# Windowed attention in a transformer kernel: the mask moved from a TensorE matmul to a VectorE addition, the maximum's subtraction to GpSimd, with new orders of work on four engines

## The chip, the cores and the metric

The kernel runs on one core of a Trainium2 chip. The metric is the device time of one execution in microseconds (us). A core has a matrix engine (TensorE; PE in the rows, PEld for its weight loads), VectorE (DVE), ScalarE (ACT), GpSimd (POOL) and SyncE (SP), which here issues the transfers. Each engine works through its own list of instructions in order; between engines only semaphores set an order.

## The reference

The input is 16 sequences of 256 tokens with 128 features. A layer norm is followed by two branches whose results are added to the input: a delta-rule mixer (untouched by the change) and a transformer of six layers, which takes most of the time. Its attention, cut to what matters (16 heads of 64, windows of 32 queries that see their own and the window before):

```python
sim = einsum('bhwie,bhwje->bhwij', bq, bk2) * QK_SCALE      # 32 queries x 64 keys a window
sim = where(mask, -finfo.max, sim)                          # mask: causal, at most 32 back, none before token 0
attn = softmax(sim, -1)
out = einsum('bhwij,bhwje->bhwie', attn, bv2)
x = attn_layer(shift_tokens(x), ...) + x
x = ffn_layer(shift_tokens(x), ...) + x
```

Queries and keys are normalised to length 1 a head and rotated before the scores are formed.

## The kernel before

`local_transformer` runs six layers over 16 sequences as one software pipeline. Each sequence of a layer is an item, and one body of the pipeline handles five items in different stages, the newest first: `new`, `turn`, `att`, `out`, `ffn`. `pipeline` calls the engine's `body` 16 times a layer and four times at the end. What each engine does in a body, and in which order, is a list written out by hand in that engine's `body` function; a step that waits holds everything behind it in the list.

The steps, by stage:

- Projection: `query_key` multiplies the item by a 512-wide piece of the weights, chunks 0 to 7, each as three matmuls into the one bank `ps_proj` (L1402). VectorE rotates it with two multiplications (`rotate` part 0 and 1, L1228 and L1235), ScalarE squares it (`square`, L1066), and only then may TensorE write chunk c + 1. VectorE sums the squares (`sum_squares`, L1243), GpSimd adds the two halves of the rotation (`add`, L987).
- Norms: when all eight chunks are summed, `inverse_roots` makes the inverse square roots on VectorE for the queries and keys of one item and for the layer norm of another at once: two preparing operations (L1292, L1295) and eleven Newton steps, one waiting for the other (`newton_step`, L61 to L69). GpSimd multiplies by them (`scale`, L997), TensorE turns the result (`turn_qk`, L1437), ScalarE copies it out (`turned_out`, L1077). `spread` on TensorE (L1527) hands the layer norm's roots out over the partitions, and `deviate`, `affine` and `ffn_in` follow it.
- Values: `value` makes four projections (pieces n = 0 to 3) into the bank `ps_p`, `value_out` copies each to the buffer `v` (L1088). After the fourth, SyncE issues 16 transfers that spread `v` over windows into `vw` (`window`, L935). There is one `v`: `value_out(x, before, 0)` of the next item waits until all 16 transfers of the item before have landed (semaphore `vw_in`).
- Attention: an item has four units. `score` writes a unit's scores into one of two banks: first a matmul of the identity by the mask (L1448), which writes the mask into the bank, then 32 small products accumulated onto it (L1454, 64 instructions in the trace). VectorE takes the negated maximum from the bank (`top`, L1251) and adds it while it copies the scores to the SBUF buffer `pr` (`shift`, L1260). ScalarE takes the exponential (`exp`, L1097), VectorE the sum and its reciprocal (`total`, L1269 and L1272), GpSimd normalises (`norm`, L1006), TensorE turns the probabilities (`turn_probs`, L1469, bank `ps_p`), ScalarE copies them (`probs_out`, L1106), TensorE multiplies by the values (`weigh`, L1487), ScalarE copies that out (`heads_out`, L1115).
- Rest of the layer: `join_heads` (L1502), `attended` (L1279), `shift_state` (L1124), `mean` (L1510), `centre` (L1286), `square_centred` (L1132), `variance` (L1518), then `spread`, `deviate`, `affine`, `ffn_in` (L1541), `gelu` (L1148), `hidden` (L1317), `ffn_out` (L1550), `layer_out` (L1325).

ScalarE's `gelu` and the first `exp` behind it each load their function table (ACT_TABLE_LOAD). Three bodies a layer also convert weights (`b.switch` of -2, -1 and 1).

## Time and profile before

| | us |
|---|---|
| median of 3 runs | 4424.85 (4423.68 to 4428.69) |
| profiled execution | 4430.44 |
| its span, first to last instruction | 4428.3 |

| engine | busy us | share of the span |
|---|---|---|
| PE | 4003.8 | 90% |
| PEld | 3348.1 | 76% |
| DVE | 3420.2 | 77% |
| ACT | 2492.3 | 56% |
| POOL | 2303.8 | 52% |

The share of busy time is an average over the span. The first projection of the transformer starts 729.1 us after the span's start and the last at 4338.6 us, so about 3,600 us belong to the pipeline described above and the first 700 us to the mixer.

### The profile page before, as it was taken

Reading aid. Unit: us, or ns where it says so; the run is one execution under the profiler, and the core shown is the slowest. Engines: PE = TensorE matmul, PEld = TensorE weight load, DVE = VectorE, ACT = ScalarE, POOL = GpSimd, SP = SyncE. Lnnn points to the kernel's source line nnn. Section 1 sums busy time; section 2 is a strip of 40 time slices with the busy share of each in tenths; the row PEclk is TensorE's granted clock in tenths of the full one; section 3 lists DMA queues with packets and bytes.
Section 4 is the critical chain, followed back from the end, with each engine's and each line's share of the span. In section 5 each row is a group of like instructions: output and inputs, shape, how many; then the busy total and the mean of one; then the engine's idle time right before and its main releaser. Section 6 shows DMA issues by size and latency. Waiting matters only on the chain. (4 is left out here: it accounts for less than half of the span.)

```text
span 4428.3 us, 165233 instructions
## 1 busy us (share of the span) xinstructions
PE 4003.8 (90%) x71312; PEld 3348.1 (76%) x71312; DVE 3420.2 (77%) x6567; ACT 2492.3 (56%) x4423; POOL 2303.8 (52%) x2141
## 2 busy tenths in 40 slices
PE   4746743899999999999999999999999999999997
PEld 4635531688888888878888888888788888888885
DVE  4376565788888888888888888888888888888883
ACT  2322211466666666666666666666666666666663
POOL 1000002566656666666666666666666665666661
PEclk9766655899999999999999999999999999999998
DMA  1000000222222222222222222222222222222222
GB/s 57 22 12 12 2 12 34 71 56 56 56 56 57 71 56 57 56 57 71 56 56 56 56 66 71 56 56 56 66 71 56 56 56 53 64 55 57 53 57 64
DMA packets 133868, 232.99 MB, mean 53 GB/s; under 512 B 26640, under 2 KB 36624, under 8 KB 131472
## 3 DMA queue, kind: packets, MB, share of 16 engines
q1 hardware_dynamic: 133136, 222.32, 20.6%
q8 instruction: 571, 9.36, 1.0%
q14 instruction: 161, 1.32, 0.1%
HBM read 29.28 MB, written 4.19 MB: 8 GB/s over the span
## 5 line engine op out<-in xcount | busy, mean ns | idle before, releaser
L987 POOL TENSOR_TENSOR qk<-rot_a,rot_b 128x512 f32<-128x512 f32 x768 | 983.5, 1285 | 418.7 <-PE bank L1437 378.2
L997 POOL TENSOR_TENSOR qk<-qk,rn 128x512 f32<-128x512 f32 x768 | 801.5, 1049 | 216.0 <-DVE rn L69 206.1
L1487 PEld LDWEIGHTS bank<-pT,vw 64*64 64x64 f32 x24576 | 752.3, 136 | 100.5 <-issue 99.5
L1487 PE MATMUL bank<-pT,vw 64*64 64x32 f32 x24576 | 794.9, 220 | 0.7 <-ACT pT L1106 0.7
L1006 POOL TENSOR_TENSOR pr<-pr,prec 128x512 f32<-128x512 f32 x384 | 400.2, 1042 | 706.1 <-DVE prec L1272 705.9
L1228 DVE TENSOR_TENSOR rot_a<-bank,rot 128x512 f32<-128x512 f32 x768 | 529.4, 689 | 297.6 <-PE bank L1402 296.4
L1066 ACT ACTIVATE sq<-bank 128x512 f32<-128x512 f32 x768 | 457.5, 596 | 470.4 <-DVE rot_b L1235 465.0
L1402 PE MATMUL bank<-w_hi,xs_hi 128*128 128x512 f32 x1152 | 555.3, 482 | 77.7 <-ACT sq L1066 28.2
L1243 DVE TENSOR_REDUCE ss<-sq 128x8 f32<-128x512 f32 x768 | 509.6, 664 | 139.0 <-ACT sq L1066 139.0
L1235 DVE TENSOR_TENSOR rot_b<-bank,rot 128x512 f32<-128x512 f32 x768 | 522.9, 681 | 0.0
L1437 PE MATMUL bank<-ident,qk 128*128 128x128 f32 x3072 | 472.6, 277 | 4.9 <-POOL qk L997 4.7
L1402 PE MATMUL bank<-w_hi,xs_lo 128*128 128x512 f32 x1152 | 461.8, 401 | 0.0
L1402 PE MATMUL bank<-w_lo,xs_hi 128*128 128x512 f32 x1152 | 460.5, 400 | 0.0
L1454 PEld LDWEIGHTS bank<-kT,qT 64*32 64x32 f32 x24576 | 363.5, 107 | 116.8 <-issue 116.7
L1437 PEld LDWEIGHTS bank<-ident,qk 128*128 128x128 f32 x3072 | 386.1, 145 | 81.5 <-POOL qk L997 9.3
L1454 PE MATMUL bank<-kT,qT 64*32 64x64 f32 x24576 | 426.9, 219 | 1.2 <-issue 0.9
L1088 ACT ACTIVATE v<-bank 128x512 f32<-128x512 f32 x384 | 229.1, 597 | 278.3 <-PE bank L1402 274.2
L1502 PE MATMUL bank<-oT,wo 128*128 128x256 f32 x1536 | 347.2, 379 | 0.7 <-ACT oT L1115 0.7
L1106 ACT ACTIVATE pT<-bank 128x512 f32<-128x512 f32 x384 | 229.2, 597 | 192.2 <-PE bank L1469 192.2
L1077 ACT ACTIVATE kT<-bank 128x512 f32<-128x512 f32 x384 | 228.1, 594 | 191.9 <-PE bank L1437 191.2
L1402 PEld LDWEIGHTS bank<-w_hi,xs_hi 128*128 128x128 f32 x1152 | 221.2, 192 | 137.0 <-issue 52.1
L1502 PEld LDWEIGHTS bank<-oT,wo 128*128 128x128 f32 x1536 | 291.5, 190 | 43.3 <-ACT oT L1115 0.8
(238 smaller groups left out, 6724.6 us busy)
## 6 DMA issues: line engine op xcount, KB each, us to landing
vw<-v SPq DMA_DIRECT2D x1344, 128.0 KB
vw<-v SPq DMA_DIRECT2D x192, 64.0 KB
stage<-in_wqkv SPq DMA_DIRECT2D x6, 1536.0 KB, 6.1
stage<-in_wb_all SPq DMA_DIRECT2D x6, 1088.0 KB, 5.3
d_band<-in_band SPq DMA_DIRECT2D x8, 512.0 KB, 5.3
d_xt<-in_x SPq DMA_DIRECT2D x4, 512.0 KB, 4.1
base_scratch<-d_res SPq DMA_DIRECT2D x4, 512.0 KB, 3.0
o_base<-base_scratch SPq DMA_DIRECT2D x1, 2048.0 KB, 8.4
```

Of the source, the lines that this page charges most:

```text
L987: nc.gpsimd.tensor_tensor(qk[:, c, :], rot_a[:, c % 2, :], rot_b[:, c % 2, :], ALU.add)\
L997: nc.gpsimd.tensor_tensor(y, y, rn[:, x.q, 8 * c:8 * c + 8].unsqueeze(2).to_broadcast([P, 8, DH]), ALU.mult).then_inc(S["scaled"], 1)
L1006: nc.gpsimd.tensor_tensor(y, y, prec[:, k % 2, :].unsqueeze(2).to_broadcast([P, NPAIR, KEYS]), ALU.mult).then_inc(S["normed"], 1)
L1066: nc.scalar.activation(sq[:, :], ps_proj[:, :], ACT.Square).then_inc(S["squared"], 1)
L1228: nc.vector.tensor_tensor(rot_a[:, c % 2, :].rearrange("p (h d) -> p h d", h=8), ps_proj[:, :].rearrange("p (h d) -> p h d", h=8), cos, AL ...
L1235: nc.vector.tensor_tensor(rot_b[:, c % 2, :].rearrange("p (h a d) -> p h a d", h=8, a=2), y[:, :, ::-1, :], sin, ALU.mult).then_inc(S["rot ...
L1243: nc.vector.tensor_reduce(ss[:, 8 * c:8 * c + 8], sq[:, :].rearrange("p (h d) -> p h d", h=8), AX.X, ALU.add).then_inc(S["summed"], 1)
L1402: mm = nc.tensor.matmul(out[:, :], x[:, q, half * P:(half + 1) * P], w[:, cols:cols + CK], start=n == 0, stop=n == 2)
L1437: mm = nc.tensor.transpose(ps_turn[:, i * P:(i + 1) * P], qk[:, c, i * P:(i + 1) * P], ident[:, :])
L1454: mm = nc.tensor.matmul(bank[w * WIN:(w + 1) * WIN, h * KEYS:(h + 1) * KEYS], qT[rows, x.q, h, q0:q0 + WIN], kT[rows, x.q, h, q0:q0 + KEYS ...
L1487: mm = nc.tensor.matmul(ps_o[rows, c * P + w * WIN:c * P + (w + 1) * WIN], vw[rows, x.q, 4 * half + w, first:first + DH], pT[rows, k % 2, ...
L1502: mm = nc.tensor.matmul(ps_c[:, 0:L], wo[:, c, :], oT[:, x.q, c, :], start=c == 0, stop=c == NPAIR - 1)
```

## The change

The mask is no longer written by a matmul. The first small product of `score` overwrites the bank. A new VectorE step `masked` adds the mask (now in SBUF, 128 x 64, repeated for eight heads) to the scores while copying them to `pr`; `top` takes the negated maximum from `pr`; `shift` moves to GpSimd, where it adds the negated maximum to `pr` in place. `score` waits for `masked` of the unit that had the bank before, where it waited for `shift`.

Beside that the lists of all four compute engines are in a new order, and the ends of the bodies lie elsewhere: the last chunk's rotation, `centre` and `inverse_roots`, which opened VectorE's body, now close the body before; ScalarE's `shift_state`, `square(7)`, `square_centred` and the fourth `value_out` do likewise, and TensorE scores unit 0 of `turn` at the end of a body in place of unit 0 of `att` at its start. The identity in bfloat16 is dropped with its preparation. The diff, cut to its core:

```diff
@@ -997,6 +995,15 @@
                 nc.gpsimd.tensor_tensor(y, y, rn[:, x.q, 8 * c:8 * c + 8].unsqueeze(2).to_broadcast([P, 8, DH]),
                                         ALU.mult).then_inc(S["scaled"], 1)
 
+            def shift(x, k):
+
+                if not x.there:
+                    return
+                need(pool, S["maxed"], x.u * 4 + (k + 1))
+                y = pr[:, k % 2, :, :]
+                nc.gpsimd.tensor_tensor(y, y, negmax[:, k % 2, :].unsqueeze(2).to_broadcast([P, NPAIR, KEYS]),
+                                        ALU.add).then_inc(S["shifted"], 1)
+
             def norm(x, k):
 
...
@@ -1012,25 +1019,29 @@
                     low_half(new, "added", turn.u * 8 + 7)
                 else:
                     low_half(new, "prepared", NPREP)
-                scale(att, 7)
+                shift(out, 3)
                 scale(turn, 0)
-                scale(turn, 1)
                 add(turn, 7)
                 add(new, 0)
+                scale(turn, 1)
                 scale(turn, 2)
+                shift(att, 0)
+                norm(out, 3)
                 add(new, 1)
+                norm(att, 0)
                 scale(turn, 3)
-                norm(out, 3)
+                add(new, 2)
+                shift(att, 1)
+                add(new, 3)
                 scale(turn, 4)
-                add(new, 2)
-                norm(att, 0)
-                add(new, 3)
                 norm(att, 1)
                 scale(turn, 5)
                 add(new, 4)
+                shift(att, 2)
+                scale(turn, 6)
                 add(new, 5)
                 norm(att, 2)
-                scale(turn, 6)
+                scale(turn, 7)
                 add(new, 6)
 
...
@@ -1150,16 +1161,6 @@
 
             def body(b):
                 new, turn, att, out, ffn = b.items
-                shift_state(ffn)
-                square(turn, 6)
-                heads_out(out, 0)
-                probs_out(out, 1)
-                turned_out(att, 5)
-                square_centred(ffn)
-                value_out(att, out, 3)
-                if b.switch == -1:
-                    convert(b, (4, 5), (S["v_projected"], turn.u * 4))
-                square(turn, 7)
                 if b.switch == -2:
                     convert(b, (0, 2, 1, 3), (S["projected"], new.u * 8))
                 high_half(b, new)
@@ -1168,38 +1169,48 @@
                     need(act, S["wo_done"], out.u)
                     nc.scalar.activation(wo[:, :, :].rearrange("p c n -> p (c n)"), stage_wo, ACT.Copy)\
                         .then_inc(S["conv_act"], 1)
-                turned_out(att, 6)
+                if b.switch == -1:
+                    convert(b, (4, 5), (S["v_projected"], turn.u * 4))
+                probs_out(out, 2)
                 heads_out(out, 1)
-                probs_out(out, 2)
                 turned_out(att, 7)
+                affine(ffn)
                 square(new, 0)
                 turned_out(turn, 0)
+                exp(out, 3)
+                gelu(ffn)
+                square(new, 1)
+                value_out(turn, att, 0)
+                exp(att, 0)
+                turned_out(turn, 1)
+                square(new, 2)
+                probs_out(out, 3)
                 heads_out(out, 2)
-                affine(ffn)
-                exp(out, 3)
-                turned_out(turn, 1)
-                square(new, 1)
-                gelu(ffn)
                 turned_out(turn, 2)
-                square(new, 2)
-                value_out(turn, att, 0)
-                probs_out(out, 3)
-                exp(att, 0)
+                value_out(turn, att, 1)
                 square(new, 3)
+                probs_out(att, 0)
+                exp(att, 1)
                 turned_out(turn, 3)
-                exp(att, 1)
-                heads_out(out, 3)
-                value_out(turn, att, 1)
-                turned_out(turn, 4)
                 square(new, 4)
-                probs_out(att, 0)
-                square(new, 5)
-                exp(att, 2)
                 value_out(turn, att, 2)
                 if b.switch == 1:
                     need(act, S["y_done"], ffn.u + 1)
                     nc.scalar.activation(w1[:, :, :, :].rearrange("p a c n -> p (a c n)"), stage_w1, ACT.Copy)\
                         .then_inc(S["conv_act"], 1)
+                heads_out(out, 3)
+                turned_out(turn, 4)
+                square(new, 5)
+                exp(att, 2)
+                heads_out(att, 0)
+                square(new, 6)
+                probs_out(att, 1)
+                turned_out(turn, 5)
+                shift_state(out)
+                value_out(turn, att, 3)
+                square(new, 7)
+                square_centred(out)
+                turned_out(turn, 6)
 
             pipeline(body)
...
@@ -1243,23 +1254,24 @@
                 nc.vector.tensor_reduce(ss[:, 8 * c:8 * c + 8], sq[:, :].rearrange("p (h d) -> p h d", h=8),
                                         AX.X, ALU.add).then_inc(S["summed"], 1)
 
-            def top(x, k):
-
-                if not x.there:
-                    return
+            def masked(x, k):
+
+                if not x.there:
+                    return
+                half, e = unit(k)
                 need(dve, S["scored"], x.u * 4 + (k + 1))
-                nc.vector.tensor_reduce(negmax[:, k % 2, :], ps_s[k % 2][:, :].rearrange("p (h n) -> p h n", h=NPAIR),
-                                        AX.X, ALU.max, negate=True).then_inc(S["maxed"], 1)
-
-            def shift(x, k):
-
-                if not x.there:
-                    return
-                need(dve, S["maxed"], x.u * 4 + (k + 1))
                 need(dve, S["p_turned"], x.u * 4 + (k - 1))
                 nc.vector.tensor_tensor(pr[:, k % 2, :, :], ps_s[k % 2][:, :].rearrange("p (h n) -> p h n", h=NPAIR),
-                                        negmax[:, k % 2, :].unsqueeze(2).to_broadcast([P, NPAIR, KEYS]), ALU.add)\
-                    .then_inc(S["shifted"], 1)
+                                        mask[:, half, :].unsqueeze(1).to_broadcast([P, NPAIR, KEYS]), ALU.add)\
+                    .then_inc(S["masked"], 1)
+
+            def top(x, k):
+
+                if not x.there:
+                    return
+                need(dve, S["masked"], x.u * 4 + (k + 1))
+                nc.vector.tensor_reduce(negmax[:, k % 2, :], pr[:, k % 2, :, :], AX.X, ALU.max, negate=True)\
...
@@ -1327,11 +1339,6 @@
 
             def body(b):
                 new, turn, att, out, ffn = b.items
-                centre(ffn)
-                rotate(turn, 7, 0)
-                rotate(turn, 7, 1)
-                sum_squares(turn, 7)
-                inverse_roots(turn, ffn)
                 if b.switch == -2:
                     need(dve, S["loaded_a"], b.layer * 32 + 32)
                     need(dve, S["rotated"], new.u * 16)
...
-                rotate(new, 0, 0)
-                top(out, 3)
-                rotate(new, 0, 1)
                 if b.switch == -1:
                     convert(b, (4, 5), 4)
+                rotate(new, 0, 0)
                 deviate(ffn)
-                shift(out, 3)
+                rotate(new, 0, 1)
+                masked(att, 0)
+                top(att, 0)
                 sum_squares(new, 0)
                 rotate(new, 1, 0)
                 rotate(new, 1, 1)
                 total(out, 3)
                 sum_squares(new, 1)
-                top(att, 0)
+                hidden(ffn)
                 rotate(new, 2, 0)
-                shift(att, 0)
                 rotate(new, 2, 1)
+                total(att, 0)
+                sum_squares(new, 2)
+                rotate(new, 3, 0)
+                rotate(new, 3, 1)
+                masked(att, 1)
                 top(att, 1)
-                hidden(ffn)
-                rotate(new, 3, 0)
-                sum_squares(new, 2)
-                rotate(new, 3, 1)
-                shift(att, 1)
-                total(att, 0)
                 sum_squares(new, 3)
                 rotate(new, 4, 0)
+                masked(att, 2)
                 rotate(new, 4, 1)
...
-                total(att, 1)
                 sum_squares(new, 4)
                 rotate(new, 5, 0)
                 rotate(new, 5, 1)
                 top(att, 2)
-                shift(att, 2)
                 sum_squares(new, 5)
-                if b.switch == 1:
-                    need(dve, S["conv_dve"], b.layer * 2 + 2)
-                attended(out)
+                masked(att, 3)
                 rotate(new, 6, 0)
                 rotate(new, 6, 1)
                 total(att, 2)
                 sum_squares(new, 6)
+                if b.switch == 1:
+                    need(dve, S["conv_dve"], b.layer * 2 + 2)
+                attended(out)
+                rotate(new, 7, 0)
+                rotate(new, 7, 1)
+                centre(out)
+                top(att, 3)
+                sum_squares(new, 7)
+                inverse_roots(new, out)
 
             pipeline(body)
...
@@ -1443,17 +1455,15 @@
                     return
                 half, e = unit(k)
                 need(pe, S["turned_out"], x.u * 8 + (4 * half + 4))
-                need(pe, S["shifted"], x.u * 4 + (k - 1))
+                need(pe, S["masked"], x.u * 4 + (k - 1))
                 bank = ps_s[k % 2]
-                nc.tensor.matmul(bank[:, :].rearrange("p (h n) -> p h n", h=NPAIR), ident_b[:, :],
-                                 mask[:, half, :].unsqueeze(1).to_broadcast([P, NPAIR, KEYS]), start=True, stop=True)
                 rows = slice(e * DH, (e + 1) * DH)
                 for h in range(NPAIR):
                     for w in range(4):
                         q0 = half * P + w * WIN
                         mm = nc.tensor.matmul(bank[w * WIN:(w + 1) * WIN, h * KEYS:(h + 1) * KEYS],
                                               qT[rows, x.q, h, q0:q0 + WIN], kT[rows, x.q, h, q0:q0 + KEYS],
-                                              start=False, stop=True, skip_group_check=True)
+                                              start=True, stop=True, skip_group_check=True)
                 mm.then_inc(S["scored"], 1)
...
@@ -1553,48 +1563,48 @@
             def body(b):
                 new, turn, att, out, ffn = b.items
                 query_key(b, new, 0)
-                turn_qk(att, 7)
+                value(b, turn, 0)
+                spread(ffn)
+                score(att, 1)
+                turn_qk(turn, 0)
+                ffn_in(ffn, 1)
+                ffn_in(ffn, 0)
+                query_key(b, new, 1)
                 weigh(out, 2)
-                spread(ffn)
-                turn_qk(turn, 0)
-                score(att, 0)
-                query_key(b, new, 1)
+                ffn_in(ffn, 2)
                 turn_qk(turn, 1)
-                ffn_in(ffn, 0)
-                ffn_in(ffn, 1)
-                value(b, turn, 0)
                 query_key(b, new, 2)
+                score(att, 2)
                 turn_qk(turn, 2)
-                score(att, 1)
-                ffn_in(ffn, 2)
+                turn_probs(out, 3, turn, 0)
+                query_key(b, new, 3)
+                value(b, turn, 1)
+                ffn_out(ffn)
+                turn_probs(att, 0, turn, 1)
+                query_key(b, new, 4)
                 turn_qk(turn, 3)
-                query_key(b, new, 3)
-                turn_probs(out, 3, turn, 0)
-                ffn_out(ffn)
                 weigh(out, 3)
-                query_key(b, new, 4)
-                value(b, turn, 1)
+                value(b, turn, 2)
+                score(att, 3)
+                query_key(b, new, 5)
                 turn_qk(turn, 4)
-                score(att, 2)
-                turn_probs(att, 0, turn, 1)
-                query_key(b, new, 5)
+                weigh(att, 0)
+                turn_qk(turn, 5)
+                turn_probs(att, 1, turn, 2)
+                query_key(b, new, 6)
                 join_heads(b, out)
-                turn_qk(turn, 5)
-                query_key(b, new, 6)
-                value(b, turn, 2)
-                weigh(att, 0)
-                turn_probs(att, 1, turn, 2)
+                query_key(b, new, 7)
+                value(b, turn, 3)
                 if b.switch == 1:
                     need(pe, S["conv_act"], b.layer * 2 + 2)
                     need(pe, S["conv_dve"], b.layer * 2 + 2)
                 mean(out)
-                query_key(b, new, 7)
-                value(b, turn, 3)
+                score(turn, 0)
+                turn_qk(turn, 6)
                 variance(out)
-                turn_qk(turn, 6)
                 turn_probs(att, 2, turn, 3)
+                turn_qk(turn, 7)
                 weigh(att, 1)
-                score(att, 3)
 
             pipeline(body)
```

## Rows read from the trace of the kernel before

**Rows 1.** Busy time in a stretch: us, then busy us and count by engine, PEclk.

```profile
1660.00:2220.00 560.00, 553.99 (x9570) 466.06 (x9566) 463.92 (x902) 362.55 (x650) 354.01 (x329) 0.99 0.25 59
```

**Rows 2.** Timeline of TensorE: start us, duration us, line, operation; `spread` of two consecutive bodies.

```profile
2151.08 0.71 PE L1527 MATMUL bank<-ident,rn 128*128 128x128 f32 x4
...
2187.88 0.71 PE L1527 MATMUL bank<-ident,rn 128*128 128x128 f32 x4
```

**Rows 3.** Line L1169 (once a layer): shortest/median/longest ns, first and last start.

```profile
L1169 ACT ACTIVATE wo<-stage x5: 1057/1057/1057, 1433.3 to 3829.6; 128x1024 f32<-128x1024 f32 x5
```

**Rows 4.** Timeline of TensorE in one body, each block from its start to the next.

```profile
2162.11 1.56 PE L1550 MATMUL bank<-hid,w 128*128 128x256 f32 x6
2163.60 2.06 PE L1487 MATMUL bank<-pT,vw 64*64 64x32 f32 x64
2165.59 0.50 PE L1402 MATMUL bank<-w_hi,xs_hi 128*128 128x512 f32 x1
...
2167.09 0.60 PE L1437 MATMUL bank<-ident,qk 128*128 128x128 f32 x4
2167.52 0.38 PE L1448 MATMUL bank<-mask,ident_b 128*128 128x512 bf16 x1
2167.83 1.10 PE L1454 MATMUL bank<-kT,qT 64*32 64x64 f32 x64
2168.86 0.66 PE L1469 MATMUL bank<-ident,pr 128*128 128x128 f32 x4
...
2170.05 3.62 PE L1502 MATMUL bank<-oT,wo 128*128 128x256 f32 x16
2173.50 0.60 PE L1437 MATMUL bank<-ident,qk 128*128 128x128 f32 x4
```

**Rows 5.** Timeline of VectorE: the `shift` of one unit.

```profile
2152.34 0.68 DVE L1260 TENSOR_TENSOR pr<-bank,negmax 128x512 f32<-128x512 f32 x1
```

**Rows 6.** Costliest groups on the page: busy us, mean ns of one | idle before.

```profile
L1006 POOL TENSOR_TENSOR pr<-pr,prec 128x512 f32<-128x512 f32 x384 | 400.2, 1042 | 706.1 <-DVE prec L1272 705.9
```

**Rows 7.** Timeline of TensorE and VectorE: projection of chunk 7, last Newton step.

```profile
2178.15 0.58 PE L1402 MATMUL bank<-w_hi,xs_hi 128*128 128x512 f32 x1
...
2186.86 0.23 DVE L69 SCALAR_TENSOR_TENSOR rn<-rn_t,rn 128x66 f32<-128x66 f32 x1
```

**Rows 8.** Timeline of GpSimd and VectorE: Newton steps beside GpSimd's work and without.

```profile
2182.35 0.72 POOL L975 TENSOR_TENSOR xs_lo<-stateT,xs_hi 64x256 fp32r<-64x256 f32 x1
...
2182.43 0.69 DVE L61 TENSOR_SCALAR rn_t<-ss 128x66 int32<-128x66 int32 x1
...
1913.96 0.20 DVE L61 TENSOR_SCALAR rn_t<-ss 128x66 int32<-128x66 int32 x1
...
1915.74 0.65 DVE L69 SCALAR_TENSOR_TENSOR rn<-rn_t,rn 128x66 f32<-128x66 f32 x1
```

**Rows 9.** Timeline of SyncE: the 16 transfers of `window`, in two bodies.

```profile
2143.76 14.10 SPq L935 DMA_DIRECT2D vw<-v  x16
...
2217.34 11.85 SPq L935 DMA_DIRECT2D vw<-v  x16
```

**Rows 10.** Short stretches behind them, columns as Rows 1, then DMA share and GB/s.

```profile
2159.00:2159.40 0.40, 0.40 (x44) 0.40 (x32) 0.40 (x2) 0.33 (x1) 0.40 (x2) 1.00 0.31 72
2159.40:2160.38 0.98, 0.98 (x20) 0.81 (x9) 0.98 (x2) 0.50 (x2) 0.98 (x2) 1.00 0.00 0
...
2230.75:2235.00 4.25, 4.25 (x84) 3.43 (x83) 3.62 (x7) 3.24 (x7) 4.24 (x4) 1.00 0.00 0
```

**Rows 11.** Timeline of ScalarE: `value_out` of piece 0, a table load, the next-but-one operation.

```profile
2160.38 0.59 ACT L1088 ACTIVATE v<-bank 128x512 f32<-128x512 f32 x1
...
2162.89 1.28 ACT L1097 ACT_TABLE_LOAD   x1
...
2164.72 0.58 ACT L1066 ACTIVATE sq<-bank 128x512 f32<-128x512 f32 x1
```

**Rows 12.** A stretch at a change of layer, columns as Rows 10.

```profile
1920.00:1921.00 1.00, 0.38 (x1) 0.41 (x2) 1.00 (x2) 0.00 (x0) 1.00 (x1) 0.50 0.86 201
```

14 lines of the change are left out of this document (7 added, 7 removed).

## The prediction

> **What bounds the kernel now.** I read the busy time of a long stretch first. In 560 us of the pipeline TensorE is busy for 554 us at a granted clock of 0.99, VectorE for 464, ScalarE for 363, GpSimd for 354 [rows 1]. So TensorE sets the time, and what counts is how long one body keeps it. Next, two consecutive starts of `spread`: they lie 36.80 us apart [rows 2], and ordinary bodies repeat that number. A layer takes (3829.6 - 1433.3) / 4 = 599.1 us [rows 3], which is 16 x 36.80 = 588.8 us and 10.3 us for the change of weights. Then the timeline of one body block by block [rows 4]: each block of TensorE begins where the last one lets it, with no wait between them. The present order is thus limited by TensorE's work alone, and every other wait in the profile is cover. The question is whether this stays so.
>
> **What the change removes.** In front of each of the 4 units of a body the mask matmul goes. From its start to the start of the scores behind it are 0.31 us [rows 4]. Not all of that is its own. The six 512-wide matmuls of two projections start 1.50 / 6 = 0.25 us apart, and that includes what the first one waits [rows 4]; the mask is as wide. Some 0.21 us are the matmul, and 0.10 us the passage from full tiles to the narrow tiles of the scores, which the kernel still makes. So 4 x 0.21 = 0.85 us leave a body, and TensorE's own work falls to 35.95 us; the other end is 4 x 0.31 = 1.24 us, 35.6 us. My sum of the new list by the blocks of [rows 4] gives 36.1 us. I use 36.0.
>
> **What it adds and moves.** VectorE: `masked` reads a bank and one SBUF operand and writes 128 x 512, as `shift` did at 0.68 us [rows 5], so it costs the same; `top` reads SBUF in place of a bank, also some 0.68 us. Where the two stand side by side the second waits for the first, 0.1 us each, twice a body in place of once. GpSimd gains 4 subtractions of one operand by a broadcast one, the form of `norm` at 1.04 us [rows 6]: 4.2 us a body, on an engine that is busy for 354 / 560 x 36.80 = 23.3 us. It ends at 27.4 of 36, so it is no bound; `exp` gets its scores about a microsecond later, and I find no matmul waiting for that. All of this is cover and costs nothing on the path. The dropped identity saves one copy in the preparation, under 1 us.
>
> The price lies in the new lists. I walk the new body with t = 0 at the start of the projection of chunk 7 on TensorE.
>
> First, **the Newton steps.** `spread` waits for `inverse_roots`. Before, from the projection of chunk 7 (2178.15) to the end of the last Newton step (2186.86 + 0.23) are 8.94 us, and `spread` starts at 2187.88 [rows 2, 7], 0.79 us later: free. In the new order VectorE has the same rotations, `centre` behind them and one reduction more (`top(att, 3)`), partly in the wait for the square; I get 9.05 us. TensorE meanwhile gets to `spread` earlier: chunk 7 0.89, value 0.70, mean 0.53, score 1.03, turn 0.43, variance 0.43, turned probabilities 0.41, turn 0.53, weigh 1.99, chunk 0 0.80, value 0.70, together 8.4 us ([rows 4], with 0.10 for each passage to narrow tiles; 0.89 and 0.53 are my estimates for a projection and a mean beside full 4-byte matmuls). It waits 0.6 us a body. What stretches the Newton steps is GpSimd: L61 takes 0.69 us beside GpSimd's operation that starts 0.08 us before it, 0.20 us with GpSimd idle, and L69, elsewhere 0.23 us, takes 0.65 us beside GpSimd [rows 7, 8]. In the new list the same three GpSimd operations (two halves of `low_half`, then `shift(out, 3)` for `scale(att, 7)`) fall on the Newton steps, so their delay of some 1.8 us stays. If it did not, 9.05 would be 7.2 and the wait would vanish; if it grew by one operation, the wait would be 1.6 us. The Trainium skill (SBUF — State Buffer, Who interferes with whom) says that GpSimd shares a port pair with VectorE, that a VectorE instruction with two SBUF inputs or in a two-port mode is locked out for the whole of a GpSimd instruction, and that one with at most one SBUF input is not. By that rule, the trace agrees (0.20 against 0.69 us), `masked` and `top` take no harm from the four new GpSimd operations.
>
> Second, **the transfers of the values.** `value_out` of the fourth piece ends and SyncE starts 2143.76 - (2178.15 - 36.80) = 2.4 us after chunk 7 [rows 2, 7, 9]; in the new list this step has the same neighbours, so again at 2.4. The 16 transfers need until 2159.40 in one body (15.6 us after the start: DMA share 0.31 before, 0.00 behind) and until 2230.75 at the latest in another (13.4 us) [rows 9, 10]. Seven successive bodies that I read this way lie between 13.0 and 15.6 us, these two near the ends; the middle is 14.1. `value_out` of the next item's first piece overwrites `v` and waits for them. Before, it starts at 2160.38 [rows 11], 16.6 us after SyncE's start: just covered. In the new list it stands two places further ahead, behind `square(new, 1)`; the walk brings ScalarE there at t = 15.6 (`spread` 9.1, `deviate` and `affine` to 10.9, `gelu` with its load to 15.1, `square` to 15.7). The transfers land at t = 2.4 + 14.1 + 0.1 = 16.6. [...]
>
> Behind the waiting `value_out` on ScalarE stand the table load for `exp`, `exp(att, 0)`, `turned_out(turn, 1)` and `square(new, 2)`. From the start of `value_out`: 0.6, then from the load to the operation behind `exp` 1.83 us (2162.89 to 2164.72) [rows 11], then 0.6 for `turned_out`, 3.1 us with the hand-over. TensorE needs it for `turn_qk(turn, 2)`, which so starts at t = 16.6 + 3.1 = 19.7. From there TensorE's list runs through to the next chunk 7: turn 0.43, turned probabilities 0.41, chunk 3 and value 1.50, `ffn_out` 1.49, turned probabilities and chunk 4 1.19, turn 0.53, weigh 1.99, value 0.90, score 1.03, chunk 5 0.80, turn 0.53, weigh 1.99, turn 0.43, turned probabilities and chunk 6 1.19, `join_heads` 3.45, together 17.9 us [rows 4]. The body closes at 19.7 + 17.9 = 37.6 us. That loop passes by the Newton wait, so the two are not added. With transfers of 13.0 us it would be 36.5 (then the next bound holds), with 15.6 us 39.1.
>
> If the transfers were in time, the loop over the Newton steps would hold: 36.0 + 0.6 for `spread`, and a further 0.2 to 0.3 for chunk 3, since its square comes behind exp's table load. That is near 36.9; I write 37.0.
>
> **The sum.** 37.6 - 36.8 = 0.8 us in about 90 ordinary bodies is +72 us. The bodies with a change of weights hide these waits behind their own (TensorE stands before chunk 0 and then runs at half its clock [rows 12]), some 1 us less a layer: -6 us. The filling and draining of the pipeline I take as unchanged. 4430.4 + 66 = 4496 us for the profiled execution. This lies 5.6 us above the median of the runs, so the forecast for the median is 4424.85 + 66 = 4491 us.
>
> **The rivals.**
> (1) Forecast, the transfers of the values are not in time and ScalarE waits: 4491 us, its own range 4450 to 4560 us by the bounds of the transfers. For it: the place moves ahead by 3.4 us where 1.0 to 3.6 us were free. Chance 0.50.
> (2) Not slower: nothing waits, TensorE's work alone counts. This needs the Newton steps at under 8.4 us (GpSimd's three operations beside other work) and transfers of at most 13 us or an earlier start. Then 36.0 to 36.3 us a body, -0.5 to -0.8 us in 96 bodies: 4345 to 4377 us. For it: TensorE runs without a wait now, and the mask's time is truly taken away. Against it: both walks. Chance 0.21.
> (3) Only the Newton wait: 37.0 us a body, +18 - 6 = +12 us, 4437 us, 4415 to 4449. Chance 0.20.
> (4) The clock falls. At a change of layer the granted clock is 0.50, 1.2 of 2.4 GHz, after TensorE stood for 4.5 us [rows 12]; if waits of about a microsecond did that in each body, some 4.5 us more a body would give about 4890 us. Over a long stretch with small gaps it was 0.99 [rows 1]. Chance 0.04.
> (5) The change does not shorten the softmax: exp comes a GpSimd operation later and TensorE waits at the turned probabilities too, 0.3 us more a body, 4520 us. Chance 0.05.
>
> **How the numbers follow.** The likeliest is (1), 4491 us. The range, 4350 to 4550 us, leaves out (4), the end of (1) with transfers of over 15 us in every body, and the fast end of (2), about 0.15 together. A measurement here tells 0.2% (9 us) from no change, so 4416 to 4434 is "same": half of (3), little of the others, 0.12. Faster: (2) and a little of (3), 0.22. Slower: 0.66.
>
> **What the profile of the changed kernel would show.** Starts of `spread` 37.6 us apart (36.0 for (2), 37.0 for (3)). TensorE idle before `turn_qk`, put down to ScalarE's copy, about a microsecond a body, and ScalarE idle before `value_out` of piece 0 with a transfer as releaser; TensorE idle before `spread`, put down to L69's successor, about 0.6 us. No L1448; scores still about 0.1 us behind a full tile. GpSimd's busy time up by 384 x 1.04 = 400 us, VectorE's unchanged within 20 us. Newton steps of up to 1 us in the middle of the chain. The prediction is wrong if the transfers start earlier than 2.4 us after chunk 7 or take less time, if VectorE gets through the Newton steps between GpSimd's operations, or if a block of TensorE costs otherwise in its new neighbourhood.

## The result and the profile after

| | before | after |
|---|---|---|
| median of 4 runs, us | 4426.77 (4423.68 to 4430.06) | 4510.94 (4503.61 to 4517.69) |
| span of the profiled execution, us | 4428.3 | 4512.5 |
| ordinary body, us | 36.80 | 37.55 |
| layer, us | 599.1 | 612.8 |

The kernel is slower: ratio 1.019, 95% interval 1.017 to 1.021. The forecast was 4491 us and 37.6 us a body. Where the body gets its length is another matter, and most of what follows is about that.

Busy time of the stretch of [rows 1], same columns:

```profile
1660.00:2220.00 560.00, 540.82 (x9350) 450.77 (x9351) 460.46 (x888) 361.16 (x637) 404.92 (x378) 0.98 0.25 60
```

TensorE is busy for 13 us less than before, at nearly the same clock (0.98, before 0.99): it waits now. GpSimd has 51 us more in it. The whole span, on the page of after, against VectorE's 3420.2 and GpSimd's 2303.8 us before:

```profile
PE 4001.3 (89%) x70928; PEld 3320.9 (74%) x70928; DVE 3461.4 (77%) x6567; ACT 2527.5 (56%) x4423; POOL 2702.8 (60%) x2524
```

Two starts of `spread` (now L1537), as in [rows 2]; the brackets give the idle time before it and what ended it:

```profile
2169.53 0.71 PE L1537 MATMUL bank<-ident,rn 128*128 128x128 f32 x4 [0.85 <-DVE rn L69]
...
2207.08 0.71 PE L1537 MATMUL bank<-ident,rn 128*128 128x128 f32 x4 [0.85 <-DVE rn L69]
```

They are 37.55 us apart, and in front of each TensorE is idle until the last Newton step. Before, `spread` stood there with no wait. The layer, as in [rows 3]: (3889.2 - 1437.9) / 4 = 612.8 us.

```profile
L1170 ACT ACTIVATE wo<-stage x5: 1057/1057/1057, 1437.9 to 3889.2; 128x1024 f32<-128x1024 f32 x5
```

The waits between 1200 and 4300 us (who waited <- for whom: total us, times, longest us) say which one repeats in each body. PEld and PE are the weight load and the matmul of the same operation, so their two waits are one:

```profile
PEld bank L1537 <- DVE rn L69: 91.8, 71, 1.6
...
PE bank L1537 <- DVE rn L69: 60.9, 71, 1.1
...
PEld bank L1520 <- ACT xf L1136: 33.7, 75, 0.5
...
PEld bank L1414 <- ACT sq L1077: 19.5, 63, 0.7
...
ACT v L1099 <- DMA vw<-v: 8.4, 17, 2.2
```

The Newton steps hold `spread` 71 times. The transfers, on which the forecast stood, hold `value_out` only 17 times, 8.4 us in all.

Now the chain that ends in `spread`, in the body that begins at 2159.63 with the projection of chunk 7 (t = 0). TensorE, GpSimd and VectorE, in order of time within each:

```profile
2159.63 0.58 PE L1414 MATMUL bank<-w_hi,xs_hi 128*128 128x512 f32 x1
...
2163.84 1.27 POOL L985 TENSOR_TENSOR qk<-rot_a,rot_b 128x512 f32<-128x512 f32 x1 [3.04 <-PE bank L1449]
2165.26 0.72 POOL L973 TENSOR_TENSOR xs_lo<-stateT,xs_hi 64x256 fp32r<-64x256 f32 x1
2166.06 0.63 POOL L975 TENSOR_TENSOR xs_lo<-stateT,xs_hi 64x255 fp32r<-64x255 f32 x1
2166.77 1.04 POOL L1004 TENSOR_TENSOR pr<-pr,negmax 128x512 f32<-128x512 f32 x1
...
2164.34 0.83 DVE L61 TENSOR_SCALAR rn_t<-ss 128x66 int32<-128x66 int32 x1
2165.20 0.20 DVE L63 TENSOR_SCALAR rn<-rn_t 128x66 int32<-128x66 int32 x1
2165.43 0.64 DVE L65 TENSOR_TENSOR rn_t<-rn 128x66 f32<-128x66 f32 x1
2166.11 0.67 DVE L67 SCALAR_TENSOR_TENSOR rn_t<-rn_t,ss 128x66 f32<-128x66 f32 x1
2166.81 1.08 DVE L69 SCALAR_TENSOR_TENSOR rn<-rn_t,rn 128x66 f32<-128x66 f32 x1
...
2169.25 0.23 DVE L69 SCALAR_TENSOR_TENSOR rn<-rn_t,rn 128x66 f32<-128x66 f32 x1
```

Four of the first five Newton steps take 0.64 to 1.08 us, where a step that GpSimd doesn't delay takes 0.20 to 0.23. Each long one lies beside one of four GpSimd operations. I had counted three (the two halves of `low_half` and the new subtraction). The fourth is `add(new, 6)`, L985: it overwrites piece 6 of `qk`, so it waits until `turn_qk(turn, 6)` has read the old one, and GpSimd stands idle for 3.04 us until then. It starts at 2163.84, half a microsecond ahead of the first Newton step. The last step ends at t = 9.85.

The transfers of the same body, and `value_out` of the next item's first piece:

```profile
2162.03 11.09 SPq L934 DMA_DIRECT2D vw<-v  x16
...
2176.14 0.59 ACT L1099 ACTIVATE v<-bank 128x512 f32<-128x512 f32 x1
```

SyncE starts at t = 2.40. ScalarE comes to `value_out` at t = 16.51 and waits for nothing. The DMA share is 0.00 from 2175.50 on, so the traffic was over 0.6 us before.

A second difference lies in the bodies with a change of weights. TensorE waited there once a layer, for 4.1 to 4.5 us; now it waits for 3.8 us and, a body later, for another 2.24 us. In each of these waits the granted clock falls to its lower level, 1.2 of 2.4 GHz, and stays there for 4 to 11 us. The second wait, and the stretch behind it (columns as [rows 10]):

```profile
1976.58 0.76 PE L1414 MATMUL bank<-w_hi,xs_hi 128*128 128x512 f32 x1 [2.24 <-DVE w_lo L1227]
...
1975.50:1986.00 10.50, 9.42 (x85) 7.85 (x86) 5.85 (x10) 4.18 (x7) 6.99 (x6) 0.51 0.73 205
```

It is `value` of piece 0, which now stands second in TensorE's body. In such a body it needs weights that VectorE converts (L1227), and VectorE comes to that only behind the Newton steps: with those shortened, as in the first experiment below, the wait falls to 0.5 us.

### The profile page after: what moved, and what is told of

Read it like the earlier page. It is cut to its first block and busy times, and to the rows that moved or that the text cites. A ratio compares the mean times of both kernels' runs of the same rounds, so it can differ in the third digit from the quotient of the medians.

```text
span 4512.5 us, 164941 instructions
## 1 busy us (share of the span) xinstructions
PE 4001.3 (89%) x70928; PEld 3320.9 (74%) x70928; DVE 3461.4 (77%) x6567; ACT 2527.5 (56%) x4423; POOL 2702.8 (60%) x2524
## 5 line engine op out<-in xcount | busy, mean ns | idle before, releaser
L985 POOL TENSOR_TENSOR qk<-rot_a,rot_b 128x512 f32<-128x512 f32 x768 | 985.3, 1283 | 488.2 <-PE bank L1449 465.5
L1414 PE MATMUL bank<-w_hi,xs_hi 128*128 128x512 f32 x1152 | 568.4, 493 | 86.9 <-POOL xs_lo L975 25.3
L1449 PE MATMUL bank<-ident,qk 128*128 128x128 f32 x3072 | 490.7, 283 | 17.5 <-ACT kT L1088 11.7
L1004 POOL TENSOR_TENSOR pr<-pr,negmax 128x512 f32<-128x512 f32 x384 | 402.9, 1049 | 54.8 <-DVE negmax L1273 35.2
L1449 PEld LDWEIGHTS bank<-ident,qk 128*128 128x128 f32 x3072 | 349.2, 142 | 102.4 <-issue 33.9
L1108 ACT ACTIVATE pr<-pr 128x512 f32<-128x512 f32 x384 | 241.9, 630 | 173.9 <-POOL pr L1004 172.8
L1088 ACT ACTIVATE qT<-bank 128x512 f32<-128x512 f32 x384 | 230.2, 600 | 192.7 <-PE bank L1449 192.7
L1264 DVE TENSOR_TENSOR pr<-bank,mask 128x512 f32<-128x512 f32 x384 | 262.2, 683 | 94.3 <-PE bank L1479 94.3
```

The lines of the kernel that those rows point to most:

```text
L985: nc.gpsimd.tensor_tensor(qk[:, c, :], rot_a[:, c % 2, :], rot_b[:, c % 2, :], ALU.add)\
L1004: nc.gpsimd.tensor_tensor(y, y, negmax[:, k % 2, :].unsqueeze(2).to_broadcast([P, NPAIR, KEYS]), ALU.add).then_inc(S["shifted"], 1)
L1414: mm = nc.tensor.matmul(out[:, :], x[:, q, half * P:(half + 1) * P], w[:, cols:cols + CK], start=n == 0, stop=n == 2)
L1449: mm = nc.tensor.transpose(ps_turn[:, i * P:(i + 1) * P], qk[:, c, i * P:(i + 1) * P], ident[:, :])
```

## The experiments

Theory A: the Newton steps, stretched by GpSimd, hold `spread`; the transfers come behind. Theory B, the forecast's: the transfers set the body. Theory C: neither waits by itself, the new order of TensorE costs more. The texts quoted below tell their own theories where there are others. Each kernel's ratio is against the kernel before, on the same chip.

**Newton steps out of GpSimd's way.** From the kernel after: `y` and the first shift live in free columns of a PSUM bank, and no step has more than one SBUF input; the same eleven steps, with the multiplications of a step in another order.

```diff
+        if k == 0:
+            ins = nc.vector.tensor_scalar(tp.bitcast(I32), x.bitcast(I32), 1, None, ALU.arith_shift_right)
...
+        elif k % 3 == 2:
+            ins = nc.vector.scalar_tensor_tensor(t, yp, -0.5, x, ALU.mult, ALU.mult)
+        elif k % 3 == 0:
+            ins = nc.vector.tensor_tensor(t, t, yp, ALU.mult)
```

> The changed kernel with one edit: the eleven Newton steps get at most one SBUF input each (the iterate y and the first shift lie in free columns of the bank ps_c, and y * x comes before the second product), so that GpSimd cannot hold them up; same count of steps, same order of work. Theory A (Newton chain: four GpSimd operations stretch it to 9.85 us after the projection of chunk 7, and spread waits 1.0 us in every body of 37.55 us): the chain takes some 3 us in place of 5.14, the wait before spread goes, a body falls to 36.4 to 36.5 us, or to about 36.9 where the transfers of the values come next; 4511 - 60 to 4511 - 105, so 4406 to 4451 us. Theory B (the transfers of the values set the body, as forecast): no change, 4511 us within 10. Theory C (the new softmax itself, with a GpSimd operation between maximum and exponential, holds TensorE up): no change.

Measured: 4493.27 us (4487.48 to 4498.55), ratio 1.0128 (1.0106 to 1.015). The wait of `spread` is gone, but ordinary bodies now take 36.4 to 40.4 us, half of them over 37.5. The waits of the same stretch:

```profile
ACT v L1117 <- DMA vw<-v: 98.0, 72, 2.8
...
PE bank L1468 <- ACT kT L1106: 92.0, 71, 2.8
```

With the first bound gone the second holds at once: `value_out` waits for the transfers 72 times, and behind it `turn_qk` (L1468) waits for ScalarE's copy, just the chain that the forecast describes. So the Newton wait was real, and taking it away alone moves the ratio from 1.019 to 1.0128, not below 1.

**Half the transfers.** From the kernel after: 8 of the 16 transfers, so part of the windows stays unwritten.

```diff
-                        for c in range(4):
-                            n = 1 if a == 0 and c == 3 else 2
+                        for c in range(2):
+                            n = 2
```

> The changed kernel with half of the value transfers left out (8 of 16 an item; the windows behind them keep what they held, so this part of the attention is not computed). Theory B: the wait before value_out was what set the body; transfers of 6 to 7 us remove it and a body falls from 37.55 to the Newton bound of about 36.9 us, 4450 us. Theory A: only the 19 waits seen before value_out (9.9 us in all) go, partly: 4500 to 4511 us.

Measured: 4491.5 us (4489.84 to 4508.36), ratio 1.0122 (1.0103 to 1.0141); an ordinary body still 37.5 us, and the wait of `spread` unchanged:

```profile
PEld bank L1537 <- DVE rn L69: 92.0, 71, 1.6
```

Theory B would have had the body shorten to about 36.9 us. It doesn't. The ratio lies below the 1.019 of after by 0.7%, more than the vanished DMA waits account for; the profiled span (4506.2 us) is only 6 us shorter.

**Both edits together**, the Newton steps with PSUM and 8 of the 16 transfers:

> The changed kernel with Newton steps of one SBUF input each and half of the value transfers left out (that part of the attention is not computed). Theory AB (two bounds stand close behind each other: the Newton chain at 37.5 us a body, and behind it the transfers of the values, which then hold value_out in most bodies, 98 us in all): with both gone a body falls to 36.4 to 36.6 us (TensorE's own 36.05 and the small waits for mean and chunk 3), 4400 to 4420 us beside 4490 with the Newton steps alone. Theory A alone (whatever made the bodies of that run vary is not the transfers): 4480 to 4500 us.

Measured: 4388.97 us (4387.48 to 4391.52), ratio 0.9905 (0.9888 to 0.9921); body 36.42 us. Each edit alone leaves the kernel 1.2 to 1.3% slower than before, both together make it 1% faster. Two bounds that lie so close behind one another look like this.

**Piece by piece for the transfers.** The same bound, lifted with all the work kept. The transfers of the left part read only piece 0 of `v`; each half gets its own semaphore, and pieces 0 and 1 of the next item wait for their own half. First on top of the Newton edit:

```diff
-                                .then_inc(S[f"vw_in{x.q}"], 16)
+                                .then_inc(S[("vw_left" if r == 0 else "vw_in") + str(x.q)], 16)
...
-                if n == 0:
-                    need(act, S[f"vw_in{before.q}"], 256 * (before.h + 1))
+                if n < 2:
+                    need(act, S[("vw_left" if n == 0 else "vw_in") + str(before.q)], 128 * (before.h + 1))
```

> The changed kernel with Newton steps of one SBUF input each, and with the transfers counted on two semaphores an item: value_out of piece 0 waits only for the 8 transfers that read the columns of that piece (issued first), piece 1 for the other 8. All transfers are made, and the whole result is computed. Theory AB: the wait before piece 0 goes, since 8 transfers are over after some 7 us; piece 1 comes 6 us later and waits for nothing. A body of 36.4 to 36.6 us, 4400 to 4420 us, that is 0.2 to 0.8% under the kernel before. Theory A alone: 4480 to 4500 us.

Measured: 4379.02 us (4369.2 to 4381.42), ratio 0.9884 (0.9867 to 0.99): faster than both kernels, with the reference's whole work. Body 36.43 us, no wait of `spread` but one of 0.2 us, and none for a transfer. The Newton steps in it, with the GpSimd operations that fall on them:

```profile
2186.05 0.23 DVE L79 TENSOR_SCALAR bank<-ss 128x66 int32<-128x66 int32 x1
...
2186.97 0.72 POOL L991 TENSOR_TENSOR xs_lo<-stateT,xs_hi 64x256 fp32r<-64x256 f32 x1
2187.10 0.23 DVE L87 SCALAR_TENSOR_TENSOR bank<-rn_t,bank 128x66 f32<-128x66 f32 x1
...
2188.67 0.22 DVE L87 SCALAR_TENSOR_TENSOR rn<-rn_t,bank 128x66 f32<-128x66 f32 x1
```

`add(new, 6)` runs here too (from 2185.55), and the two halves of `low_half`; the eleven steps take 2188.89 - 2186.05 = 2.84 us, where the kernel after needs 2169.48 - 2164.34 = 5.14. The Trainium skill (SBUF — State Buffer, Who interferes with whom) would have it so: an instruction of VectorE with at most one SBUF input, outside the two-port modes, is not locked out by GpSimd. The trace agrees, with 0.22 to 0.23 us for each step beside GpSimd's operations. One SBUF input alone isn't enough, though: the first step (`L61`) had only one before as well and took 0.83 us. The edit also moved its output to the bank; whether it was in a two-port mode before, no run here shows.

Theory C falls with this run: TensorE's new order, with both waits gone, takes 36.43 us a body, less than the old one.

**The semaphores alone**, from the kernel after:

> The changed kernel with the split semaphores alone, Newton steps as they are. Theory A (the Newton chain is the first bound, the transfers only the second): the body stays at 37.51 us and only the 19 single waits before value_out go, 0 to 15 us of 4511. Theory B (transfers set the body): 4450 us or less.

Measured: 4498.24 us (4487.75 to 4499.34), ratio 1.0144 (1.0116 to 1.0172). No DMA wait is left, the body is 37.51 us, and `spread` waits as before:

```profile
PEld bank L1538 <- DVE rn L69: 93.1, 72, 1.6
```

That is half the transfers' result again, with nothing left out: the transfers are not the first bound.

**The fourth operation earlier.** In the kernel after, `turn_qk(turn, 6)` before `score(turn, 0)` on TensorE, so that `add(new, 6)` starts a microsecond sooner:

```diff
-                score(turn, 0)
                 turn_qk(turn, 6)
+                score(turn, 0)
```

> The changed kernel with two neighbours exchanged in TensorE's list: turn_qk(turn, 6) before score(turn, 0). GpSimd's add(new, 6) waits for that turn; it starts 1.0 us earlier and ends before the first Newton step, which now takes 0.83 us beside it. Theory A: the first Newton step falls to 0.20 us, the chain by 0.6 us, a body to about 36.95 us, 4511 - 55 = 4456 us. Theories B and C: no change, 4511 us.

Measured: 4499.44 us (4491.26 to 4513.41), ratio 1.0135 (1.0114 to 1.0157); half of the ordinary bodies take up to 37.4 us, a quarter over 37.7, and in the profiled execution nothing is gained (span 4511.3 us against 4512.5, a layer 613.0). Much less than expected, for two reasons that the rows show: `add` is over before the Newton steps now, but the two halves of `low_half` begin just with them (they wait for ScalarE's copy `xs_hi`), so the first step is as long as before; and the transfers hold in 45 cases.

```profile
2156.90 1.27 POOL L985 TENSOR_TENSOR qk<-rot_a,rot_b 128x512 f32<-128x512 f32 x1 [1.86 <-PE bank L1449]
2158.60 0.73 POOL L973 TENSOR_TENSOR xs_lo<-stateT,xs_hi 64x256 fp32r<-64x256 f32 x1 [0.43 <-ACT xs_hi L1069]
...
2158.62 0.77 DVE L61 TENSOR_SCALAR rn_t<-ss 128x66 int32<-128x66 int32 x1
...
PEld bank L1537 <- DVE rn L69: 71.1, 71, 1.0
...
ACT v L1099 <- DMA vw<-v: 40.2, 45, 2.6
```

The wait of `spread` fell by 92 - 71 = 21 us in 71 bodies, 0.3 us each: in this body the eleven steps take 2163.35 - 2158.62 = 4.73 us in place of 5.14, about what they took before the change with three operations beside them, 2187.09 - 2182.43 = 4.66 us [rows 7, 8]. I had put the whole 0.63 us of the first step down to `add`; with `add` gone, another GpSimd operation takes its place on that step, and only the number of operations that hit the chain counts.

**What the mask matmul is worth.** From the fast version above, with the mask matmul put back in front of the scores and all products accumulating onto it again (VectorE still adds the mask as well, so the mask counts twice):

```diff
+                nc.tensor.matmul(bank[:, :].rearrange("p (h n) -> p h n", h=NPAIR), ident_b[:, :],
+                                 mask[:, half, :].unsqueeze(1).to_broadcast([P, NPAIR, KEYS]), start=True, stop=True)
```

> The fastest version so far (changed kernel, Newton steps of one SBUF input, split semaphores, 36.43 us a body, ratio 0.988) with the mask matmul put back in front of the scores; masked adds the mask a second time, which changes nothing in the result. Theory: that version is bound by TensorE, and a mask costs 0.21 us: 36.43 + 0.85 = 37.28 us, 4380 + 82 = 4462 us. With 0.31 us each 37.67 us, 4499 us. If waits of other engines bound it, less than 0.4 us a body more.

Measured: 4435.24 us (4429.69 to 4444.49, 10 runs), ratio 1.0007 (0.9997 to 1.0018); body 37.24 us, 0.81 us more. TensorE in it:

```profile
1807.93 0.39 PE L1481 MATMUL bank<-mask,ident_b 128*128 128x512 bf16 x1
...
1808.25 1.10 PE L1487 MATMUL bank<-kT,qT 64*32 64x64 f32 x64
```

From the mask to the scores are 0.32 us again, and the block in front of it becomes 0.09 to 0.10 us shorter, as the passage to narrow tiles moves behind the mask: 0.22 us net for each, where the forecast had 0.21; the body gives 0.81 / 4 = 0.20. The whole time grew less than expected: the ratio by 0.0123, some 55 us for 82, and the profiled span by 4439.7 - 4367.1 = 72.6 us.

**The matmul left out of the kernel before**, which then computes without a mask:

> The kernel before with the mask matmul left out and nothing in its place (the scores aren't masked, so that part of the result isn't computed). It measures what the mask matmul takes of TensorE's time. With 0.21 us each, as forecast: 35.95 us a body, 4432 - 82 = 4350 us. With 0.31 us each: 35.56 us, 4313 us. With another wait behind it (the Newton chain has 0.79 us left there, of which one mask lies in it): not under 36.3 us.

Measured: 4395.56 us (4383.67 to 4415.2, 7 runs), ratio 0.9924 (0.9899 to 0.9949); body 36.20 us, 0.60 less instead of 0.85, and the ratio some 34 us lower instead of 82. Part of the gain goes to a wait that the mask had covered, `turn_qk` for GpSimd's scaled half:

```profile
PEld bank L1437 <- POOL qk L997: 28.9, 140, 0.6
```

**The Newton edit in the kernel before**, where I saw the chain covered:

> The kernel before with only the Newton steps changed to one SBUF input each. The chain gets some 1.8 us shorter, but there it ends 0.79 us before spread already, so it is cover: 36.80 us a body, no change within 0.2%. If the Newton chain had bound the kernel before too, 0.3 us a body or more would go, under 4400 us.

Measured: 4415.74 us (4411.65 to 4425.96, 10 runs), ratio 0.9957 (0.9943 to 0.9972). The ordinary body is unchanged at 36.8 us, as expected. But a layer takes (3812.1 - 1423.3) / 4 = 597.2 us instead of 599.1: at a change of weights, where one body took 43.97 us and takes 42.47, the chain did count. The expectation missed that, and its "no change within 0.2%" with it.

**The new softmax in the order of before.** `masked` in the old place of `top`, `top` in that of `shift`, GpSimd's subtraction ahead of `norm`, TensorE's list untouched but for the mask:

```diff
-                top(att, 0)
+                masked(att, 0)
...
-                shift(att, 0)
+                top(att, 0)
```

> The kernel before, in its own order of work, with the new softmax: no mask matmul, masked on VectorE where top stood, top where shift stood, shift on GpSimd put into its list before norm(out, 3), norm(att, 0) and norm(att, 2), and for out 3 behind scale(turn, 1). Theory A: the Newton chain keeps its three GpSimd operations and spread its place behind a weigh, so nothing waits there; TensorE's work alone counts, 36.80 - 0.85 = 35.95 us a body, 4427 - 80 = 4347 us (up to 4380 where single waits appear). Theory B: value_out keeps its late place, same number. Theory C: the new softmax costs by itself, 4430 to 4510 us.

Measured: 4862.22 us (4850.52 to 4892.39), ratio 1.0971 (1.0923 to 1.102); body 40.85 us. I expected less than before and got 10% more. The waits of its trace:

```profile
DVE pr L1266 <- PE bank L1481: 180.3, 74, 5.2
...
PE bank L1562 <- DVE hid L1331: 150.1, 74, 2.0
```

`masked` writes `pr`, as `shift` did, and must wait until `turn_probs` two units back has read it. In the place of `top`, which wrote no `pr`, it asks too early, up to 5.2 us, and `hidden` stands behind it on VectorE; `ffn_out` (L1562) waits for that.

Part of the loss is the clock. In one such body, with the granted clock behind the wait (columns as [rows 10]):

```profile
2319.09 2.93 PE L1562 MATMUL bank<-hid,w 128*128 128x256 f32 x6 [2.03 <-DVE hid L1331]
...
2319.00:2322.50 3.50, 3.41 (x20) 2.40 (x20) 3.47 (x8) 1.72 (x3) 1.00 (x2) 0.52 0.00 0
```

TensorE stands for 2.03 us, then the clock is at its lower level, and `ffn_out` takes 2.93 us where it took 1.56 [rows 4]: 1.4 of the four microseconds. Over the stretch of [rows 1] the granted clock is 0.93 instead of 0.99. This is what rival (4) of the forecast describes, in another kernel and at a third of its size.

**`masked` beside `top`, at the place of `shift`:**

> The kernel before, in its own order of work, with the new softmax, masked and top side by side where shift stood (the variant before had masked where top stood, 40.85 us a body, with VectorE waiting 180 us for the turned probabilities that free pr). Theory D (masked in top's place waits for pr, and all of VectorE's list with it): that wait goes and a body falls to 36.5 to 38 us, 4400 to 4540 us. Theory E (it is the longer way from maximum to exponential over GpSimd that holds the old order up): the body stays above 39 us.

Measured: 4558.63 us (4557.46 to 4561.87), ratio 1.0289 (1.0272 to 1.0306); body 37.77 us. It takes away three of the four microseconds, so the early place was their cause, by the wait and by the clock behind it. TensorE waits for squares now, since VectorE does two operations in a row before the next rotation:

```profile
PEld bank L1416 <- ACT sq L1079: 144.2, 151, 2.8
...
PE bank L1416 <- ACT sq L1079: 97.5, 152, 2.4
```

So in the two placings tried the new softmax gains nothing without new lists, and with those of the change it loses 1.9% in place of 2.9%.

**`score` before `mean`** in the fast version:

```diff
-                mean(out)
                 score(turn, 0)
+                mean(out)
```

> As the kernel with Newton steps of one SBUF input and split semaphores, and with score(turn, 0) ahead of mean(out) in TensorE's list. Theory AB with TensorE as the bound: the 0.18 us that mean waits for the shifted state go, since the score fills them, and the Newton chain, now some 1 us clear, takes the later mean: 0.1 to 0.2 us a body, 10 to 20 us less. If the Newton chain were close behind again, the later centre would make it 10 to 60 us more.

Measured: 4405.06 us (4402.74 to 4411.57), ratio 0.9946 (0.9928 to 0.9963); body 36.82 us, 0.39 more, where I expected less. `variance` (L1548) waits for the squared centred values, as the mean came later and nothing lies between:

```profile
PEld bank L1548 <- ACT xsq L1161: 63.3, 83, 0.8
...
PE bank L1548 <- ACT xsq L1161: 43.6, 83, 0.5
```

## Why the prediction was right or wrong

The sign, the time and the body's length came out: 4491 forecast, 4510.94 measured; 37.6 and 37.55 us. The mechanism named first did not come first. That its sum, 19.7 + 17.9, gives the body that the other wait makes, 36.08 + 1.02 + 0.45, is luck. Step by step:

- **What bounds before.** Right: TensorE's list. The Newton edit leaves the ordinary body at 36.8 us. Only in bodies with a change of weights is there something to gain, 1.9 us a layer.
- **What the matmul is worth.** Right for the ordinary body: 0.21 us forecast, 0.20 to 0.22 by the mask put back. TensorE's own work, 37.55 less the waits of 1.02 (`spread`), 0.18 (`mean`) and 0.27 us (chunk 3), is 36.08; I used 36.0.
- **GpSimd and VectorE.** GpSimd +400 forecast, 2702.8 - 2303.8 = 399.0 measured. VectorE "unchanged within 20 us" was wrong, 3461.4 - 3420.2 = +41 us: not the new operations but the longer Newton steps. With those in PSUM it is 3255.1 us, against 3276.8 for the old lists with the same edit.
- **The Newton wait.** The term that failed in size. Chain to the end of the last step 9.05 forecast, 9.85 measured; TensorE there at 8.4 and 8.88; wait 0.6 and 1.02. The mis-step is "the same three GpSimd operations": there is a fourth, `add(new, 6)`, which `turn_qk(turn, 6)` releases. The eleven steps took 5.14 us where three operations had made it 4.66 before and make it 4.73 with `turn_qk` earlier: 0.4 to 0.5 of the 0.80 missing. The other 0.3 lies ahead of them: they begin 4.71 us after chunk 7, before the change 4.28, among others because `mean` waits 0.17 us for ScalarE. TensorE's own list was sized too small as well, by 0.17 for that wait, 0.10 for `mean` and 0.16 for the turned probabilities. The prediction had this very case as a bound ("if it grew by one operation, the wait would be 1.6 us") and rejected it. With 1.02 in place of 0.6, rival (3) reads 36.08 + 1.02 + 0.45 = 37.55.
- **The transfers.** SyncE's start at 2.4 was exact. `value_out` was expected ready at 15.6 and the transfers at 16.6. ScalarE came at 16.5, because `spread` was 0.8 us late, and the transfers of most bodies were there by then (here all were issued within 11.09 us and the traffic was over 13.5 us after SyncE's start, for 14.1 in the forecast). So the Newton wait filled the time in which ScalarE would have waited for them. The statement that the loops are not added was right, and so was the rest of the loop: `turn_qk(turn, 2)` at t = 19.8 (19.7 forecast) and 17.7 us to the next chunk 7 (17.9). With the Newton wait taken away the forecast chain appears as written, 98 us in 72 waits. It was the second bound, behind the first by some tenths of a microsecond.
- **The changes of weights.** The term that failed most in microseconds. Forecast 1 us a layer in favour, since the new waits would hide behind the old one; measured 612.8 - 599.1 = 13.7 us a layer, of which the ordinary excess of 0.75 x 16 is 12.0. So these bodies lose 1.7 us a layer more. The trace shows a wait that the walk did not look for, `value` of piece 0 behind VectorE's conversion of the weights, 2.24 us, and a second stretch at the lower clock. The one old wait of 4.1 to 4.5 us became two of 3.8 and 2.24 us. In the fast version, a layer of 589.7 us, the changes of weights cost 6.8 us beyond 16 ordinary bodies, where they cost 12.0 in the kernel after and 10.3 before. Four layers carry 54.8 of the 84 us, and the other two at the same rate 27. The forecast had -6 us for all changes of weights, 1.7 us on six layers are +10: 16 of the 20 us by which it fell short. The ordinary excess came out as forecast (0.8 x 90 = 72 us against 0.75 x 96 = 72).
- **The rivals.** (2), not slower, fell to the two waits; the fast version shows what it was worth, 36.43 us a body (36.0 to 36.3 forecast). (4), the clock, did not happen in ordinary bodies: 1.00 in the one shown, with its wait of 1.02 us. At changes of weights it did. (5), probabilities late, has no wait in the list.

What stays open: why the kernels with half or split transfers lie some 0.5% below the kernel after by their ratios, when their vanished DMA waits were 8.4 us in 3100 and their profiled spans are only 6 and 15 us shorter. The kernel after was not run again on their chips, and the exchanged `turn_qk` shows the same 0.5% with a span of 1 us less, so at least part of it need not come from the edits. Open too is what an order of GpSimd's list that keeps all four operations off the Newton steps would give, which wasn't tried.

## What to carry to other kernels

When a walk through a new order finds two loops of nearly equal length, work out in thought what is left when either is gone, and when both are: here each edit alone left a loss of over 1%, both gave a gain of 1%. List every instruction of the neighbouring engine that can fall on a serial chain, those released by another engine too, and not only those that stood beside it before. A chain of small dependent steps on VectorE beside a busy GpSimd is worth trying with PSUM operands before anything else is reordered. And walk the rare bodies too, those with a change of weights: they held most of the 20 us that the forecast missed.

## What the runs showed of the hardware

The same eleven VectorE steps on 128 x 66 values, beside the same kind of GpSimd operations, took 5.14 us with SBUF operands and 2.84 us with at least one operand of each step in PSUM and at most one SBUF input; over the kernel VectorE's busy time fell by 206 us (3461.4 to 3255.1). A step that GpSimd hit took as long as what was left of GpSimd's operation: 1.08 us for `L69` beside the subtraction of 1.04, and `L61` ended 0.06 us after `add`. The granted clock after an idle time of TensorE: 1.00 after 1.02 us in an ordinary body, 0.50 after 4.5 us at a change of layer [rows 12], and either after some 2 us. It fell after 2.24 us (0.51) and after the 2.03 us in front of `ffn_out` (0.52); in the run with only the Newton edit it was 0.57 over the 4 us behind a wait of 2.33 us and 1.00 behind one of 2.26 us.
